# Causal convolution with blocks of 64: two heads in one Toeplitz buffer, products on quarters of the array

## The reference

```python
# x: (2, 2048, 128), H = 16 heads of D = 8 columns
z = jnp.einsum('bse,he->bsh', x, W_A) * SCALING
z = jax.nn.softmax(z, axis=1)                 # over time, for each head
zp = jnp.transpose(z, (0, 2, 1))
idx = (i - j) % S
roll = zp[:, :, idx] * (j <= i)               # Toeplitz and lower triangular, 2048 x 2048 for each head
v = jnp.einsum('bse,fe->bsf', x, W_V).reshape(B, S, H, D)
out = jnp.einsum('bhij,bjhd->bihd', roll, v).reshape(B, S, E)
return jnp.einsum('bse,fe->bsf', out, W_O) + b_O
```

## Time and profile before

| | |
|---|---|
| median of 3 executions | 1342.97 us (1341.92 to 1343.94) |
| profiled execution, its own time | 1346.67 us |
| its span, from the first to the last instruction | 1344.2 us |
| mean granted clock of TensorE | 0.945 of full speed |
| PE busy | 1194.4 us (89%) |
| ACT, DVE, POOL busy | 896.4, 895.0, 708.0 us |
| products of the convolution (L1618), busy | 117.5 us |

### The profile page before, as it was taken

How to read it: one execution, slowest core, us unless ns; L and a number is a source line. 1 busy time by engine, 2 the same in 40 slices (tenths; PEclk the granted TensorE clock), 3 DMA queues, 4 the chain that set the end, 5 groups by cost and what they waited for, 6 DMA issues and landing times. The chain is left out here.

```text
span 1344.2 us, 34846 instructions
## 1 busy us (share of the span) xinstructions
PE 1194.4 (89%) x11174; PEld 872.5 (65%) x11183; DVE 895.0 (67%) x2443; ACT 896.4 (67%) x3049; POOL 708.0 (53%) x1170
## 2 busy tenths in 40 slices
PE   5899984999999988978999999979967999599997
PEld 3666761566666667964666666669946999444443
DVE  4689994677777756765777777647772001479998
ACT  3578873788888867856888888857763000277776
POOL 1579975788888852316888888823264000211112
PEclk9599996999999998998999999979978999799999
DMA  6000000122111112002121111100006886100000
GB/s 209 1 2 10 10 2 14 43 50 49 41 41 33 33 25 99 0 7 47 44 60 42 41 37 33 29 1 1 0 8 213 295 284 220 32 9 14 12 14 16
DMA packets 50824, 71.29 MB, mean 53 GB/s; under 512 B 25566, under 2 KB 36762, under 8 KB 46298
## 3 DMA queue, kind: packets, MB, share of 16 engines
q1 hardware_dynamic: 50682, 69.44, 18.0%
HBM read 46.20 MB, written 2.38 MB: 36 GB/s over the span
## 5 line engine op out<-in xcount | busy, mean ns | idle before, releaser
L1145 PE MATMUL psum<-wa_wqkv,wa_hT 128*128 128x512 f32 x384 | 201.6, 611 | 0.2 <-DVE wa_tmp L1020 0.2
L1106 ACT ACTIVATE wa_p<-psum,wa_nb 128x128 f32<-128x128 f32 x512 | 180.6, 372 | 2.3 <-DVE wa_nb L1032 2.3
L1000 POOL TENSOR_TENSOR wa_p<-wa_p,wa_rrs 128x512 f32<-128x512 f32 x128 | 133.3, 1041 | 51.4 <-DVE wa_rrs L1039 51.4
L1936 PE MATMUL psum<-ex_wT,ex_hT 128*128 128x512 f32 x256 | 132.5, 599 | 0.9 <-DVE ex_yw L1875 0.3
L1961 ACT ACTIVATE ex_yw<-psum,ex_w 128x128 f32<-128x128 f32 x384 | 103.0, 398 | 40.6 <-DVE ex_total L1892 33.7
L1032 DVE TENSOR_REDUCE wa_nb<-psum 128x4 f32<-128x512 f32 x128 | 82.5, 686 | 70.4 <-PE psum L1177 70.4
L1618 PE MATMUL psum<-cv_v,cv_toep 128*128 128x128 f32 x1024 | 117.5, 277 | 6.5 <-DMA cv_toep<-cv_zpad 6.5
L1618 PEld LDWEIGHTS psum<-cv_v,cv_toep 128*128 128x128 f32 x1024 | 116.7, 194 | 6.7 <-issue 6.7
L1106 ACT ACTIVATION_READ_ACCUMULATOR wa_p<-psum,wa_nb 128x1 f32 x512 | 109.0, 213 | 0.0
L1391 PE MATMUL psum<-ml_hnT,ml_w 128*128 128x128 f32 (+1 forms) x768 | 102.5, 285 | 0.0
L1116 ACT ACTIVATE wa_pT<-psum 128x512 f32<-128x512 f32 x128 | 77.7, 607 | 34.4 <-PE psum L1154 34.4
(11 more groups left out here) (263 smaller groups left out, 3393.9 us busy)
## 6 DMA issues: line engine op xcount, KB each, us to landing
cv_toep<-cv_zpad SPq DMA_DIRECT2D x32, 1024.0 KB, 5.5
wa_vm<-wa_v SPq DMA_DIRECT2D x127, 128.0 KB, 2.3
wa_tabs<-in_rotations_dram SPq DMA_DIRECT2D x2, 2048.0 KB, 8.2
x_rows<-in_L_attn_x_dram SPq DMA_DIRECT2D x4, 512.0 KB, 6.2
out_dram<-x_rows SPq DMA_DIRECT2D x32, 64.0 KB, 1.5
wa_rows<-y_rows SPq DMA_DIRECT2D x14, 128.0 KB
wa_rows<-y_rows SPq DMA_DIRECT2D x14, 127.0 KB
wa_wqkv<-in_L_ffn_wqkv_dram SPq DMA_DIRECT2D x2, 768.0 KB, 11.4
```

Of the source, the lines that this page charges most:

```text
L1000: nc.gpsimd.tensor_tensor(p, p, cols_bc(rrs[:, t % 2, r, :], P), ALU.mult)\
L1106: e = nc.scalar.activation(pr[:, t % 2, r, h, :], sim_bank[r][:, P * h:P * h + P], ACT.Exp, bias=nb[:, t % 2, r, h:h + 1], accum_out=rs[:, ...
L1145: nc.tensor.matmul(bank, hT[:, t % 3, :], wqkv[:, INNER * k:INNER * k + INNER], start=True, stop=True).then_inc(done.sem, 1)
L1936: nc.tensor.matmul(bk[k], hT[:, u, :], wT[:, BANK * k:BANK * k + BANK], start=False, stop=True).then_inc(p_up(f"bank{k}"), 1)
```

## The change

- A block of time is now 64 rows. `cv_toep` keeps its size, but partitions 0 to 63 hold one head and partitions 64 to 127 another, eight heads on; there are 16 pairs of heads, and 32 lags of 64 rows. Two transfers of 512 KB (64 partitions each) fill one buffer.
- The product for one lag, one head and one parity of the output block (`second`: even blocks go to PSUM partitions 0 to 63, odd blocks to 64 to 127) has 64 x 64 weights. The head decides the rows of the array, the parity its columns, so that four products fall to four quarters. The two heads sum in different PSUM banks.
- Blocks ahead of time 0 are left out: the moving columns number 128 at lag 0 and fall by 8 for every two lags down to 8. The zeros in `vall` and their memset on POOL are gone.
- The values are projected as 16 products of 64 x 64 columns for each group instead of 4 of 128 x 128, since `vall` has blocks of 64 rows with one head group in each partition half.
- `keep` copies 256 columns out of two banks, 16 times instead of 32. The banks are given new numbers.
- The output products of batch 0 are mixed in after every pair from pair 9 on.

```diff
-        vall, oall = sb("cv_v", [P, B, 2, NT, E]), sb("cv_o", [P, TILES, E])
+        vall, oall = sb("cv_v", [P, B, BLOCKS, E // SIDES]), sb("cv_o", [P, TILES, E])
...
-        conv_bank, turn_bank, z_bank, v_bank = bk[0:2], bk[2:4], bk[4], bk[5:7]
+        conv_bank, z_bank, turn_bank, v_bank = c.psum[:, 0:4, 0:P], bk[3], bk[4:6], bk[6:8]
...
-                    row = bass.AP(tensor=zpad.tensor, offset=s * (P + T) + 1, ap=[[1, P], [1, T]])
-                    sp.dma_start(toep[:, u, :], row).then_inc(toep_in[u], 16)
+                    for a in range(SIDES):
+                        head = s // PER_SIDE * CH + a * PER_SIDE + s % PER_SIDE
+                        row = bass.AP(tensor=zpad.tensor, offset=head * (P + T) + HALF + 1, ap=[[1, HALF], [1, T]])
+                        sp.dma_start(toep[side(a), u, :], row).then_inc(toep_in[u], 16)
...
-                nc.gpsimd.memset(vall[:, :, 0, :, :], 0.0).then_inc(g_zero, 1)
...
-                        m = nc.tensor.matmul(v_bank[g % 2][:, P * k:P * k + P], hT[:, g % 2, k, :], wvT[:, :],
-                                             start=True, stop=True)
+                        for second in range(2):
+                            at, reversed_at = HALF * (2 * k + second), HALF * (1 - second)
+                            for a in range(SIDES):
+                                m = nc.tensor.matmul(v_bank[g % 2][side(a), at:at + HALF],
+                                                     hT[:, g % 2, k, reversed_at:reversed_at + HALF], wvT[:, side(a)],
+                                                     start=True, stop=True)
...
-                    for m in range(NT):
-                        v = vflat[:, NT - m:2 * NT - m, h * CD:h * CD + CD]
-                        mm = nc.tensor.matmul(conv_bank[s % 2][:, 0:P].rearrange("p (n d) -> p n d", d=CD),
-                                              toep[:, u, P * m:P * m + P], v, start=m == 0, stop=m == NT - 1)
+                    for lag in range(BLOCKS):
+                        for second in range(2):
+                            i = max(0, (lag - second + 1) // 2)
+                            if i == NT:
+                                continue
+                            v = 2 * i + second - lag
+                            for a in range(SIDES):
+                                to = conv_bank[side(second), SIDES * (s % 2) + a, CD * i:CD * NT]
+                                mm = nc.tensor.matmul(to.rearrange("p (n d) -> p n d", d=CD),
+                                                      toep[side(a), u, HALF * lag:HALF * lag + HALF],
+                                                      blocks[side(a), 0:NT - i, v, CD * k:CD * k + CD],
+                                                      start=lag == 0, stop=lag >= BLOCKS - 2, skip_group_check=True)
...
+                    behind = s - PER_SIDE - 1
+                    if behind == 0:
+                        pe.wait_ge(v_w, 2)
+                    if behind >= 0 and behind % 2 == 0:
+                        turn_o(behind // 2)
+                    if behind >= 0 and behind % 2 == 1:
+                        o_project(behind // 2)
                 for g in range(PER_B, GROUPS + 1):
                     if g < GROUPS:
                         turn_o(g)
-                    if g > PER_B:
-                        o_project(g - 1)
+                    o_project(g - 1)
```

More of the change, by code:

```diff
@@ L1403, in causal_convolution @@
     nc, inp, bk = c.nc, c.inp, c.bank
-    PAIRS = B * CH
+    ROWS = B * CH
+    SIDES, HALF = 2, P // 2
+    PER_SIDE = CH // SIDES
+    PAIRS = B * PER_SIDE
+    BLOCKS = T // HALF
     GT = 4
@@ L1414, in causal_convolution @@
         zs = sb("cv_z", [CH, B, T])
-        zeros = sb("cv_zeros", [PAIRS, P])
+        zeros = sb("cv_zeros", [ROWS, P])
         zpart = sb("cv_zpart", [CH, GROUPS])
@@ L1438, in causal_convolution @@
         p_oT, a_oT, p_wo, v_out = sem("p_oT"), sem("a_oT"), sem("p_wo"), sem("v_out")
-        conv_bank, turn_bank, z_bank, v_bank = bk[0:2], bk[2:4], bk[4], bk[5:7]
+        conv_bank, z_bank, turn_bank, v_bank = c.psum[:, 0:4, 0:P], bk[3], bk[4:6], bk[6:8]
         tiles_of = lambda t, g: t[:, GT * g:GT * g + GT, :]
         batch = lambda g: g // PER_B
+        side = lambda a: slice(HALF * a, HALF * a + HALF)
         backward = lambda bank: bank.rearrange("p (k t) -> p k t", t=P)[:, :, ::-1]
@@ L1466, in _ @@
                     sp.wait_ge(spread, 16 * (b + 2))
-                    for h in range(CH):
-                        fetch(b * CH + h)
+                    for k in range(PER_SIDE):
+                        fetch(b * PER_SIDE + k)
             @block.gpsimd
@@ L1551, in keep @@
                     dve.wait_ge(p_conv, s + 1)
-                    b, h = s // CH, s % CH
-                    nc.vector.tensor_copy(oall[:, b * NT:b * NT + NT, h * CD:h * CD + CD],
-                                          conv_bank[s % 2][:, 0:P].rearrange("p (n d) -> p n d", d=CD))\
-                      .then_inc(v_conv, 1)
+                    b, k = s // PER_SIDE, s % PER_SIDE
+                    to = oall[:, b * NT:b * NT + NT, :].rearrange("p n (a e) -> p a n e", a=SIDES)
+                    nc.vector.tensor_copy(to[:, :, :, k * CD:k * CD + CD],
+                                          conv_bank[:, SIDES * (s % 2):SIDES * (s % 2) + SIDES, :]
+                                          .rearrange("p a (n d) -> p a n d", d=CD)).then_inc(v_conv, 1)
                 def residual(g):
@@ L1576, in _ @@
                     keep(s)
-                    if s >= CH + 3 and (s - CH - 3) % 3 == 0 and (s - CH - 3) // 3 < PER_B:
-                        residual((s - CH - 3) // 3)
-                for g in range(PER_B, GROUPS):
+                    if s >= PER_SIDE + 3 and (s - PER_SIDE - 3) % 2 == 0:
+                        residual((s - PER_SIDE - 3) // 2)
+                for g in range(PER_B - 1, GROUPS):
                     residual(g)
@@ L1610, in convolve @@
                     u = s % RING
-                    pe.wait_ge(toep_in[u], (s // RING) * 16 + 16)
+                    pe.wait_ge(toep_in[u], 16 * SIDES * (s // RING + 1))
                     if s >= 2:
                         pe.wait_ge(v_conv, s - 1)
-                    b, h = s // CH, s % CH
-                    vflat = vall[:, b, :, :, :].rearrange("p s n e -> p (s n) e")
-                    for m in range(NT):
-                        v = vflat[:, NT - m:2 * NT - m, h * CD:h * CD + CD]
-                        mm = nc.tensor.matmul(conv_bank[s % 2][:, 0:P].rearrange("p (n d) -> p n d", d=CD),
-                                              toep[:, u, P * m:P * m + P], v, start=m == 0, stop=m == NT - 1)
+                    b, k = s // PER_SIDE, s % PER_SIDE
+                    blocks = vall[:, b, :, :].rearrange("p (n two) e -> p n two e", two=2)
+                    for lag in range(BLOCKS):
[10 more added lines that the diff above has]
+                                                      start=lag == 0, stop=lag >= BLOCKS - 2, skip_group_check=True)
                     mm.then_inc(p_conv, 1)
                 def turn_o(g):
-                    pe.wait_ge(v_conv, CH * (batch(g) + 1))
+                    pe.wait_ge(v_conv, PER_SIDE * (batch(g) + 1))
                     if g >= 2:
@@ L1692, in outputs @@
                     act.wait_ge(p_v, g + 1)
-                    nc.scalar.activation(vall[:, b, 1, GT * q:GT * q + GT, :],
-                                         v_bank[g % 2].rearrange("p (n e) -> p n e", e=E), ACT.Copy)\
+                    nc.scalar.activation(vall[:, b, 2 * GT * q:2 * GT * q + 2 * GT, :],
+                                         v_bank[g % 2].rearrange("p (n e) -> p n e", e=HALF), ACT.Copy)\
                       .then_inc(a_v, 1)
```

9 lines of the change are left out of this document (1 added, 8 removed).

## The result

The changed kernel takes 1376.58 us (median of 4 executions, 1375.88 to 1378.82) against 1342.51 us for the kernel before on the same chip (4 executions, 1341.92 to 1343.94). The ratio is 1.0256, 95% interval 1.0239 to 1.0272. It is 34 us slower, where 39.7 us of gain were predicted: the prediction was wrong, and its sum is 73 us off.

What follows compares the result with a forecast made beforehand. PE alone was taken to bound the convolution stage. Its 121.3 us fall to 80.6 us (-40.7), the tail adds 1.0, so 1342.97 - 39.7 = 1303.3 us; range 1299 to 1321 us, its own 1299 to 1311.

Steps and rivals of the forecast that it cites:

- the cost of nothing for the arrival of PE's instructions: Convolution stage on PE: the sum had no term for fetching the products' code, though they grow from 512 to 2016.
- 73.7 us for the 16 pairs: Convolution products on PE: 16 pairs of heads at 4.61 us each, where the heads took 114.2 us.
- 80.6 us: PE's convolution stage after: 73.7 pairs + 4.0 output work + 1.2 switching + 1.7 half clock, against 121.3 us.
- rival B: PE's code in the convolution arrives too slowly: 33 x 5.3 = 175 us, time 1405 us; 0.05 with C, mostly B.
- the point of loss: Convolution stage: the change becomes a loss once a piece of PE's code costs 3.4 us in all.
- Rival C: PE array: only two of four quarters work at once, 16 pairs take 147 us, time about 1377 us; 0.05 with B.
- the line of the prediction: Convolution rounds of 72 to 128 columns: interpolated from 0.058 us at 64 columns to 0.108 us at 128, averaging 0.086 us.
- Rivals A: Convolution records have a floor of their own: 1311 to 1335 us in part (0.12), 1335 us or more in full (0.05).
- the half-height transfers at no cost: Toeplitz loads: 32 of 0.5 MB need about 230 GB/s, below the sustained 289 GB/s, so 0 us added.
- the first 3.4 us were put at half clock: Start of PE's convolution stage: half clock after the first wait stays, losing 1.7 us.
- The tail: Behind the last pair: one more output group and a wider last copy add 1.0 us (0.5 to 1.6).
- The first buffer: First Toeplitz buffer: again 1 MB from one queue, landing 0 to 0.3 us later behind one more issue.

Runs made afterwards that it cites:

- e1: The changed kernel with only the first four pairs' Toeplitz buffers fetched, later pairs reusing them: 1351.4 us, ratio 1.0055 to the kernel before.
- e10: The kernel before with each product split into two of 64 weight columns on two column halves, only columns with values, full-height transfers: 1319.58 us, ratio 0.9838.
- e5_loop: The changed kernel with only the first ring fetched, one bank set, output work last, 16 pairs as a hardware loop: 1329.0 us; written out 1370.6 us.
- e7: The kernel before with each Toeplitz buffer fetched by two transfers of 64 partitions instead of one of 128: 1381.3 us.
- e3: The changed kernel with all products at 128 moving columns, same number of instructions: 1384.8 us.
- e4: The changed kernel with four heads at a time, one for each quarter, and half of the code: 1337.99 us, ratio 0.997 to the kernel before.
- e9: The changed kernel with four heads at a time, six of eight groups as three turns of a two-group loop: 1326.21 us, ratio 0.987 to the kernel before.
- e8: The changed kernel with four heads at a time, lower Toeplitz halves fetched from ACT's queue after the first ring: 1338.33 us, ratio 0.9952 to the kernel before.
- e2: The changed kernel with every product after lag 0 cut to 8 moving columns, same number of instructions: 1390.2 us.

## Why the prediction was wrong, point by point

**The failed step is the cost of nothing for the arrival of PE's instructions.** The sum has 73.7 us for the 16 pairs, as if the code were always there; the stage lasted 154.1 us in place of 80.6 us. The prediction knew the danger as its rival B. It had counted 33 pieces (there were 31 in the stage), asked for one in 2.2 us, and put the point of loss at 3.4 us a piece. It then gave B and C together a chance of 0.05, because "PE shows no gap in 30 us now, though it was never asked for this pace, and the load on the engines falls". Both halves of that sentence were true and neither is evidence. Pieces come 3.84 us apart on quiet engines (e1), above the point of loss, and 4.8 us apart with traffic. That the load falls helps little: most of the cost is a chain of steps, not bandwidth. B's own price of 5.3 us, the landing time behind rows, is near what was measured, but for another reason: 3.8 us of it are there without any rows. The trace of before could have said how far it reached: no two packets of its instruction queue start less than 7.8 us apart in the whole program, nor less than 10.6 us in this stage. A demand for one in 2.2 us lay more than three times outside everything shown, and should have had a chance near that of the forecast.

Rival C of the prediction named 1377 us, and 1376.6 us were measured. That is chance: four quarters do work at once (below).

The Trainium skill ("Runtime: NRT & Kernel Launch", section "Instruction fetch mechanics") has PE's instruction memory refilled in blocks of 256 instructions ahead of execution, hidden because instructions are dispatched more slowly than they are fetched. The size agrees (stops at every 256 records, 16 KB). Hidden it is at one block in 10.6 us or more, as in this stage before; at one in 5.6 to 6.7 us beside full DMA engines (e10) or in 3.84 us on quiet ones (e1) PE stands. The same section prefers written-out code to branches; here the loop was 41.6 us faster than its written-out twin.

**Right: the array.** Four quarters work at once; the first 17 rounds of a pair (128 to 96 columns) take 0.098 us each, which is what the line of the prediction gives for their widest members (115 columns on average), and the narrow ones 0.060 us where it had 0.058; a pair is 4.79 us of products, 0.18 us more than forecast (2.9 us over 16 pairs). Rivals A and C of the prediction are excluded by e5_loop. Had the instructions come, the mechanism would have given its gain up to the next limit.

**Wrong, hidden: the half-height transfers at no cost.** The prediction held them to the 289 GB/s of the full-height ones; "PE would wait only below 230 GB/s" was the right test, and the rate is 216 (e7). With 2 x 0.52 MB for each pair the transfers would have set the pace: 1.05 MB / 216 GB/s = 4.9 us a pair, 4 us more than forecast in all. In the changed kernel another wait covers it. How much of the 27.1 us of traffic comes from the half height was not tried.

**Not foreseen: stops cost the clock.** The change has a mean granted clock of 0.83 in the stage where only the first 3.4 us were put at half clock. As e3 shows, that doesn't set the time while pieces do; how much it adds between stops is left open.

**The ends.** The tail is right: +0.87 us (predicted +1.0). The first buffer is not: the first product comes +1.5 us later (predicted 0 to 0.3). From the first Toeplitz transfer to the first product 7.8 us pass in place of 5.8 us, and 7.5 us in e7, so it is the half-height rows again.

In sum, the stage holds the 80.6 us of the forecast, 46.4 us that are there with quiet DMA engines, and 27.1 us that come with the Toeplitz rows: 80.6 + 46.4 + 27.1 = 154.1 us. Of the 46.4 us, 2.9 us are the array's by e5; the rest goes with the stops for code and the lower clock around them.

## What to carry to other kernels

Work on parts of the array multiplies instructions. Divide the instructions of a stage (loads and products; four for each float32 product here) by 256 and compare the time for each piece with the closest distance at which the trace has shown pieces to arrive. In these runs PE stood for code when it wanted a piece more often than once in 3.8 us on quiet engines, in 4.8 us beside the half-height rows of the changed kernel (DMA share 0.44), and in about 6 us beside full-height rows at a share of 1.0. Cut the instructions then (e10_halves: two column halves with trimmed columns and full-height loads need 2.31 us of the array a head, where the four quarters need 4.79 us for two), or loop over a body that stays in place. And test a change of a transfer's height by itself: the same bytes over 64 partitions moved at 216 GB/s with the engines full, where rows over 128 partitions reached 410.

## What the runs showed of the hardware that was not expected

- Pieces of 256 instructions come 3.84 us apart on quiet engines (e1), of which the packet takes 0.9 to 1.4 us; beside full-height rows, with the engines at 1.0 most of the time, they come 5.5 to 6.7 us apart (e10, 1034 to 1083 us).
- A body of 504 instructions (e5) and one of 1024 (e9) run again and again without a new fetch; in e5 a turn came every 5.41 us to within 0.01 us.
- A piece that stands behind a burst of 2 MB of rows stops PE for 3.5 to 4.5 us (e4), and a second queue does not change that (3.3 to 4.8 us, e8).
- Rows of 8 KB into 64 partitions move at 216 GB/s with the engines at 1.02 (e7), and at 233 GB/s at 0.95 when the two halves of the partitions are written at a time from two queues (e8).
- Products of 8 columns throughout left the granted clock at 0.50 for the whole stage, products of 128 columns at 0.95, with 33.8 and 29.6 us of stops on issue (e2, e3).
